# Attention of a perceiver block: four runs of key tiles in place of three, the softmax shift copied under two score tiles of a run, a quarter of the maxima in a score bank

## What is computed

```python
x = x + _L0_xattn_ref(_layernorm(x), ctx_1024, ctx_1024, W_Q, ..., b_O)   # x (32,64,256), ctx (32,1601,256)
x = x + _L0_attn_ref(_layernorm(x), ...)      # state space scan
x = x + _L0_ffn_ref(_layernorm(x), ...)       # top 2 of 8 experts

def _L0_xattn_ref(x_q, x_k, x_v, ...):        # 16 heads of 16
    Q, K, V = (x_q @ W_Q + b_Q), (x_k @ W_K + b_K), (x_v @ W_V + b_V)   # split into heads
    scores = einsum('bhld,bhsd->bhls', Q, K) / sqrt(16)
    return einsum('bhls,bhsd->bhld', softmax(scores), V) ... @ W_O + b_O
```

## Time and profile before

| | us |
|---|---|
| median of 3 runs | 2261.07 (2260.78 to 2264.43) |
| the profiled execution: its own time / its span | 2261.17 / 2259.4 |
| PE busy in the span | 2070.6 (92%) |
| DVE busy | 1453.5 (64%) |
| ACT busy | 1249.6 (55%) |
| POOL busy | 747.9 (33%) |

### The profile page before, as it was taken

How to read it: one execution, slowest core, us unless ns; L and a number is a source line. 1 busy time by engine, 2 the same in 40 slices (tenths; PEclk the granted TensorE clock), 3 DMA queues, 4 the chain that set the end, 5 groups by cost and what they waited for, 6 DMA issues and landing times. The chain is left out here.

```text
span 2259.4 us, 65085 instructions
## 1 busy us (share of the span) xinstructions
PE 2070.6 (92%) x28676; PEld 1738.4 (77%) x28676; DVE 1453.5 (64%) x2619; ACT 1249.6 (55%) x1680; POOL 747.9 (33%) x571
## 2 busy tenths in 40 slices
PE   7999999999999999999999999688699998599993
PEld 5899999988888999999999998543133337599993
DVE  6555665555565565565565563536788874788885
ACT  3455555545555555555555555168799981366661
POOL 3232322222222222222222220000899962255551
PEclk9899999999999999999999999899899998699997
DMA  3111111111111111111111110214875530766663
GB/s 117 38 43 49 41 43 49 41 42 42 45 43 37 49 41 43 49 41 43 49 41 43 49 34 8 66 56 157 233 177 141 144 85 30 232 219 217 226 234 126
DMA packets 131138, 195.41 MB, mean 86 GB/s; under 512 B 18116, under 2 KB 109252, under 8 KB 130696
## 3 DMA queue, kind: packets, MB, share of 16 engines
q1 hardware_dynamic: 121832, 174.98, 25.8%
q0 software_dynamic: 4416, 12.06, 1.6%
q10 hardware_dynamic: 4608, 4.20, 0.6%
HBM read 159.61 MB, written 31.59 MB: 85 GB/s over the span
## 5 line engine op out<-in xcount | busy, mean ns | idle before, releaser
L560 DVE TENSOR_REDUCE max_part<-work 128x1 f32<-128x384 f32 (+1 forms) x1024 | 538.7, 570 | 304.0 <-PE work L692 278.5
L627 ACT ACTIVATE probs<-scores 128x1024 f32<-128x1024 f32 (+1 forms) x416 | 426.1, 1026 | 243.2 <-PE scores L717 222.2
L235 POOL TENSOR_TENSOR ctx_lo<-ctx_whole,ctx_hi 128x768 fp32r<-128x768 f32 (+1 forms) x128 | 232.2, 1815 | 787.4 <-DVE ctx_hi L229 787.4
L1343 POOL TENSOR_TENSOR decay<-steps_in,xn 128x1024 f32<-128x1024 f32 x126 | 243.7, 1964 | 132.9 <-POOLq L951 116.3
L555 DVE SCALAR_TENSOR_TENSOR keys_lo<-work,bk,keys_hi 128x384 fp32r<-128x384 f32 (+1 forms) x256 | 162.7, 635 | 156.4 <-ACT keys_hi L602 156.4
L602 ACT ACTIVATE keys_hi<-work,bk 128x384 fp32r<-128x384 f32 (+1 forms) x256 | 152.5, 596 | 180.2 <-PE work L672 180.2
L711 PE MATMUL scores<-q_hi,keys_hi 64*128 64x256 f32 (+1 forms) x1664 | 247.8, 288 | 2.9 <-issue 1.7
L711 PE MATMUL scores<-q_lo,keys_hi 64*128 64x256 f32 (+1 forms) x1664 | 239.6, 278 | 1.5 <-issue 1.5
L711 PE MATMUL scores<-q_hi,keys_lo 64*128 64x256 f32 (+1 forms) x1664 | 238.8, 278 | 0.0
L682 PE MATMUL work<-wv_hi,ctx_hi 128*128 128x256 f32 (+1 forms) x832 | 235.7, 283 | 1.9
L682 PE MATMUL work<-wv_hi,ctx_lo 128*128 128x256 f32 (+1 forms) x832 | 233.5, 281 | 0.0
(11 more groups left out here) (233 smaller groups left out, 4598.2 us busy)
## 6 DMA issues: line engine op xcount, KB each, us to landing
xs<-in_w_T SPq DMA_DIRECT2D x46, 1024.0 KB, 6.9
ctx_whole<-in_ctx_T SPq DMA_DIRECT2D x96, 384.0 KB, 3.2
steps_in<-scratch_results SPq DMA_DIRECT2D x256, 128.0 KB, 2.7
ctx_whole<-in_ctx_T SPq DMA_DIRECT2D x32, 449.0 KB, 3.8
scratch_results<-steps SPq DMA_DIRECT2D x16, 512.0 KB, 2.6
scratch_mixed<-mixed ACTq DMA_DIRECT2D x32, 128.0 KB, 1.7
scratch_z<-z SPq DMA_DIRECT2D x16, 256.0 KB, 3.7
zg<-scratch_z SPq DMA_DIRECT2D x16, 256.0 KB, 3.1
```

The source lines that it names most:

```text
L235: nc.gpsimd.tensor_tensor(s.ctx_lo[c][:, :, 0:n], s.ctx_whole[c % 2][:, :, 0:n], s.ctx_hi[c][:, :, 0:n].bitcast(F32), ALU.subtract).then_i ...
L560: nc.vector.reduce_max(max_part[par][:, place(pair), c:c + 1], bank[:, 0:CHUNKS[c][1]], AX) \
L627: nc.scalar.activation(probs[n % PROBS][0:rows, :], scores[slot][0:rows, :], ACT.Exp, scale=1.0 / HD ** 0.5).then_inc(exp_done, 1)
L1343: nc.gpsimd.tensor_tensor(decay[u % DS][:, :, 0:n], steps_in[t % LOADS][:, 0:1, 0:n].to_broadcast([P, 2, n]), a_rep[:, 2 * i:2 * i + 2, 0: ...
```

## The change

There are four runs now, one to a chunk: tiles 0 to 2, 3 to 5, 6 to 8, and 9 to 12. A pair of maxima stands in front of the first and the second tile of a run only. Behind the run stand the third pair and a "wide" unit: the fourth pair of maxima goes into the score bank that the run's last tile but one has left (two halves of 512 columns, which are filled whole; the chunk's first columns come from two further small matmuls in chunk 0, from the neighbouring keys in the others), and DVE reduces it in one instruction. `neg_max` is taken behind the last wide unit. Key units of chunk 1 are no longer among the first units.

The shift goes another way for 7 of the 13 tiles. At a batch's start PE writes the two shift matmuls into the bank of tile 1; ACT copies that bank into SBUF (`shift_all`), and tile 1's score adds onto it. For tiles 4, 3, 7, 6, 10 and 9 (the first two tiles of each later run) ACT copies `shift_all` into the score bank (`prefill`), and the score adds onto that; these scores wait for `prefilled` in place of the exponential. Tiles 0, 2, 5, 8, 11 and 12 have their shift matmuls as before.

The core of the diff:

```diff
-FIRST_UNITS = keys_unit(0, 0) + keys_unit(1, 0) + keys_unit(0, 1) + keys_unit(1, 1) + values_unit(0, 1)
+FIRST_UNITS = keys_unit(0, 0) + keys_unit(1, 0) + values_unit(0, 1)
 PHASES = [
-    ([0, 1, 2, 3], [maxima(0, 0, 2), maxima(0, 2, 4), maxima(0, 4, 6), maxima(0, 6, 8)],
-     maxima(1, 0, 2) + keys_unit(0, 2) + keys_unit(1, 2) + values_unit(2) + values_unit(3, 4) + values_unit(5)
-     + values_unit(6, 7)),
...
-    ([8, 9, 10, 11, 12], [maxima(2, 4, 6), maxima(2, 6, 8), maxima(3, 0, 2), maxima(3, 2, 4), maxima(3, 4, 6)],
-     maxima(3, 6, 8) + values_unit(11, 12) + [None, None, ("row",)]),
+    ([0, 1, 2], [maxima(0, 0, 2), maxima(0, 2, 4), []],
+     maxima(0, 4, 6) + wide_maxima(0, 6) + keys_unit(0, 1) + keys_unit(1, 1) + values_unit(2) + values_unit(3, 4) + [None]),
+    ([3, 4, 5], [maxima(1, 0, 2), maxima(1, 2, 4), []],
+     maxima(1, 4, 6) + wide_maxima(1, 6) + keys_unit(0, 2) + keys_unit(1, 2) + values_unit(5) + values_unit(6, 7)),
...
+    ([9, 10, 11, 12], [maxima(3, 0, 2), maxima(3, 2, 4), [], []],
+     maxima(3, 4, 6) + wide_maxima(3, 6) + values_unit(11, 12) + [("row",)]),
 ]
...
+WIDE_TILE = [tiles[-2] for tiles, _, after in PHASES if any(unit and unit[0] == "wide" for unit in after)]
+SHIFT_TILE = PHASES[0][0][1]
+PREFILLED = [t for tiles, _, _ in PHASES[1:] for t in (tiles[1], tiles[0])]
...
+            def wide_unit(b, par, u):
+                _, pairs, c = UNITS[u]
+                dve.wait_ge(wide_done, b * len(WIDE) + WIDE.index(u) + 1)
+                nc.vector.reduce_max(
...
+            def prefill(b, par, t):
+                act.wait_ge(shift_copied, b + 1)
+                act.wait_ge(exp_done, b * NT + t - 1 + CREDIT)
+                if t - 2 in WIDE_TILE and b + 1 < batches:
+                    act.wait_ge(wide_reduced, (b + 1) * len(WIDE) + WIDE_TILE.index(t - 2) + 1)
+                nc.scalar.copy(scores[(par * NT + t) % 2][:, :], shift_all[:, :]).then_inc(prefilled, 1)
+
             def attend(b, par):
+                act.wait_ge(shift_ready, b + 1)
+                nc.scalar.copy(shift_all[:, :], scores[(par * NT + SHIFT_TILE) % 2][:, :]).then_inc(shift_copied, 1)
...
+                    if tiles[-1] + 2 in PREFILLED:
+                        prefill(b, par, tiles[-1] + 2)
                     if b + 1 < batches:
                         for u in after:
                             unit(b + 1, 1 - par, u)
+                            if KIND[u] == "k" and UNITS[u][1] == KD - 1:
+                                prefill(b, par, tiles[-1] + 1)
...
+            def wide_unit(b, par, u):
+                _, pairs, c = UNITS[u]
+                bank = wide_bank(par, u)
+                if b > 0:
+                    pe.wait_ge(exp_done, (b - 1) * NT + WIDE_TILE[WIDE.index(u)] + 1 + CREDIT)
...
             def score(b, par, t):
...
-                pe.wait_ge(exp_done, b * NT + t + 1)
+                ahead = t == SHIFT_TILE or t in PREFILLED
+                if t == SHIFT_TILE:
+                    pe.wait_ge(shift_copied, b + 1)
+                elif t in PREFILLED:
+                    pe.wait_ge(prefilled, b * len(PREFILLED) + PREFILLED.index(t) + 1)
+                else:
+                    pe.wait_ge(exp_done, b * NT + t + 1)
...
+                if not ahead:
+                    last = shift(b, par, t, rows, start=False)
                 last.then_inc(scores_ready, 1)
...
             def attend(b, par):
+                wait_evacuated(pe, b, ROW)
+                pe.wait_ge(exp_done, b * NT + SHIFT_TILE + 1)
+                shift(b, par, SHIFT_TILE, P, start=True).then_inc(shift_ready, 1)
```

More of the change, by code:

```diff
@@ L424 @@
 KIND = [unit[0] if unit else None for unit in UNITS]
+IN_WORK = [kind not in (None, "wide") for kind in KIND]
+WIDE = [u for u in range(NU) if KIND[u] == "wide"]
 ROW = KIND.index("row")
 LAST_MAX = max(u for u in range(NU) if KIND[u] == "max")
+assert WIDE[-1] == LAST_MAX + 1
 WORK_BANKS = 3
-assert NU % WORK_BANKS == 0
+PLACE = [sum(kind != "wide" for kind in KIND[:u]) for u in range(NU)]
+assert sum(kind != "wide" for kind in KIND) % WORK_BANKS == 0
+WORK_OF = [n % WORK_BANKS for n in PLACE]
 BESIDE = []
@@ L438 @@
 V_UNITS = [u for u in range(NU) if KIND[u] == "v"]
-NUMBER = [sum(kind is not None for kind in KIND[:u]) for u in range(NU)]
-DONE = sum(kind is not None for kind in KIND)
-FORMER = [max(i for i in range(u + NU) if i % WORK_BANKS == u % WORK_BANKS and i < u + NU and KIND[i % NU])
+NUMBER = [sum(IN_WORK[:u]) for u in range(NU)]
+DONE = sum(IN_WORK)
+FORMER = [max(i for i in range(u + NU) if WORK_OF[i % NU] == WORK_OF[u] and i < u + NU and IN_WORK[i % NU])
           for u in range(NU)]
@@ L657, in unit @@
                     return
+                if KIND[u] == "wide":
+                    wide_unit(b, par, u)
+                    return
                 kind = KIND[u]
-                bank = work[u % WORK_BANKS]
+                bank = work[WORK_OF[u]]
                 batches_back, former = 1 - FORMER[u] // NU, FORMER[u] % NU
@@ L698, in unit, with shift @@
                 last.then_inc(unit_done, 1)
+            def shift(b, par, t, rows, start):
+                bank = scores[(par * NT + t) % 2]
+                for h in range(2):
+                    last = nc.tensor.matmul(bank[0:rows, h * BANK:(h + 1) * BANK], ones[side(h), 0:rows],
+                                            shifts[side(h), :], start=start, stop=True, skip_group_check=True)
+                return last
             def score(b, par, t):
@@ L711, in score @@
                             last = nc.tensor.matmul(bank[0:rows, at:at + GCOLS], k[par][side(g), m, start:start + rows],
[L712 removed]
+                                                    q[par][side(g), m, :], start=(m == 0 and n == 0 and not ahead),
+                                                    stop=(ahead and m == KD - 1 and n == len(parts) - 1),
                                                     skip_group_check=True)
[L714 to L718 removed]
+                if not ahead:
+                    last = shift(b, par, t, rows, start=False)
                 last.then_inc(scores_ready, 1)
```

79 lines of the change are left out of this document (53 added, 26 removed).

## The result

| | before | after |
|---|---|---|
| median, us | 2260.93 (4 runs, 2259.96 to 2264.43) | 2299.01 (4 runs, 2297.68 to 2300.02) |
| ratio | | 1.0165, 95% interval 1.0148 to 1.0183 |
| span of the profiled execution | 2259.4 | 2298.0 |

The account below looks back on a forecast made before the run. PE was taken to set the pace, waiting in hand-overs once shift pairs no longer filled them. +1.5 us a batch gave +47 over 31 steps, plus 6 for the last batch: 2261 + 47 + 6 = 2314 us, range 2270 to 2346.

Parts of the forecast that it names:

- Hand-over, third tiles: Third tiles of runs 2 to 4: 0.89 us of work against a 1.38 hand-over, waiting 0.49 each, 1.47 a batch.
- First run: Tile 1 waits 0.43 for the shift copy behind ACT's DMA issue, tile 2 0.27 more: 0.70; 0.5 without that hold.
- ACT behind a run: A score-bank write ahead of `keys_hi` delays PE behind the key units: +0.35 in run 2, +0.15 in run 1, total 0.5.
- the dear writes: Rival: ACT needs 1.5 us per write into PSUM, +0.5 each where copies bind, giving 2363 us; chance 0.04.
- A fourth run: One more change from maxima to keys, values to mixes and mixes to maxima, 0.07 to 0.1 each: +0.25 a batch.
- Row unit: At the batch's end the row unit still waits 0.9, now for DVE instead of ACT's values copy: change 0.
- The value units' wait for maxima: Value units' wait for DVE's maxima goes, since the wide unit stands between: -0.3 us a batch.
- Tile 12 and wide: Run 4's fourth tile and the wide unit behind it wait 0.24 us more, exponentials starting no closer than 0.96 apart.
- Wide maxima: Pairs of 512 columns cost 0.23 in place of 0.18, chunk 0's two further matmuls about 0.2: +0.35 a batch.
- The sum: All terms together: +1.5 us a batch, +47 over 31 steps, and +6 in the last batch from exposed ACT copies.
- The clock: Rival: PE's clock falls at each batch's end, costing 2 us a batch, giving 2376 us; chance 0.03.
- The first batch's units hold the same work, 0: The units run in the first batch hold the same work as before, so its time changes by 0.

Follow-up runs that it names:

- e4_nopre: The changed kernel with shift matmuls back in every tile and no ScalarE writes; four runs, wide maxima and pair places kept: 2286.73 us, 1.0114 of before.
- e1_third: The changed kernel with the third pair of narrow maxima of each run moved back in front of the run's third tile: 2282.69 us, 1.0096 of before.
- e3_early: The changed kernel with tile 1's shift matmuls and their copy for the next batch placed ahead of the last run's mixes: 2303.16 us, 1.0188 of before.
- e2_behind: The changed kernel with both ScalarE writes of the score banks placed behind the run's two key units: 2284.51 us, 1.0102 of before.
- e7_runs: The kernel before with four runs and chunk 1's key units moved as in the changed kernel; narrow maxima, all 13 shift pairs on PE: 2255.85 us, 0.9971.
- r1_before: The kernel before run once more, unchanged: 2265.32 us (1 run).
- r2_after: The changed kernel run once more, unchanged: 2299.29 us (1 run).
- e10_row: e7_runs with the last run's mixes and ACT's copy of `mixed` ahead of the row unit and first units: 2234.96 us, 0.9894 of before.
- e13_first: e10_row plus ScalarE writes only for each later run's first tile, behind the key units, and the copied shift made in tile 0's bank: 2244.28 us, 0.9935 of before.
- e12_wide: Changed kernel, third pair before third tile, writes behind key units, shift copy before mixes, plus wide units of runs 1 to 3 behind key units: 2291.53 us, 1.0137.

## Why the prediction came out

- *Hand-over, third tiles.* Right: 1.38 to 1.40 from a score's end to full pace on the tile two later, so a wait of 0.49, of which the list shows 0.23 and not 0.3 to 0.5. That shift pair and maxima had filled the time is shown by e4_nopre (with six shift pairs back the period is even 0.20 shorter) and e1_third (the waits at third tiles go from 114 to 4).
- *First run.* 0.70 was predicted, 0.45 + 0.21 = 0.66 measured, with the copy behind the DMA's issue. e3_early shows that the smaller figure of the prediction, 0.5 without that hold, is the floor: its third tile starts at 732.03, 1.28 behind the first score's end; with the 0.10 of its slower first pair this is the 1.38 of the hand-over alone.
- *ACT behind a run.* 0.5 predicted; 0.42 by the trace and 0.46 by e2_behind. The write was guessed at 1.0 us and takes 1.017; the dear writes fell.
- *A fourth run.* 0.25 predicted, 0.27 by e7_runs.
- *Row unit.* Right: 0.7 as before, now for `neg_max`. The value units' wait for maxima went as said, and 448 shift matmuls stand in place of 832.
- *Tile 12 and wide.* 0.24 predicted, about 0.2 found.
- *Wide maxima.* 0.35 predicted, of which 0.2 for chunk 0's two further matmuls. No run shows this term alone, but those 0.2 are too much: in e4_nopre run 1, which has them, takes 4.07 from its maxima to its keys, and run 2 takes 4.04.
- *The sum.* +1.5 a batch predicted, 43.89 - 42.28 = +1.61 measured; last batch +6 predicted, 26.34 - 20.80 = +5.5 measured (+4.4 against r1_before, whose last batch is slower; see the clock).
- *The clock.* 1.00 in the window of after, so that rival fell. The section on HAM oscillation in the Trainium skill (TensorE: Matmul & The Clock Gate) has a kernel that loses the clock at each of its waits for DMA. The batches here keep 1.00 in spite of the waits listed above, so it doesn't show in them. The 1.00 of the last batch in the earlier trace rows, which the prediction held against this rival, isn't there in every execution. Windows of r1_before, at its last batch's start:

```profile
1398.00:1401.00 3.00, 1.32 (x58) 1.04 (x47) 0.00 (x0) 0.32 (x1) 0.00 (x0) 1.00 0.00 0
1401.00:1404.00 3.00, 3.00 (x36) 2.70 (x34) 0.00 (x0) 1.88 (x3) 0.00 (x0) 0.68 0.16 49
```

Behind a stretch in which PE is busy 1.32 of 3 us the granted clock falls to 0.68; in the first profile of before PE is busy 1.52 of 3 us there, and 1.00 follows. What decides stays open.

The forecast was 15 us too high, and two steps of the total are mis-sized. "The first batch's units hold the same work, 0": the first copy of `mixed` comes at 113.7 in place of 121.5 (113.9 against 123.6 in the repetition), 8 to 10 us earlier. And the 31 steps were added to a time of before that holds more than 31 periods: in nine batches of before PE stops, 11 us together (last section), and after has almost none. The 29 steps of after are 35.9 us longer in all, which is 29 x 1.61 = 46.7 less what those stops had added; the batch behind them adds 2.0, the last 5.5, the part after the attention 3.0; less 7.8 this is the 38.6 by which the span grew. The prediction has nothing for that part. The 3.0 comes again as 2.1 in the second pair (r2_after against r1_before); over the fourteen profiles the part takes 838.7 to 841.5 in before, r1_before, e7_runs, e10_row and e13_first and 842.5 to 846.6 in the others. Whether and how the change lengthens it stays open. What the forecast's mechanism covers comes to 46.7 + 2.0 + 5.5 = 54.2, close to the 53 forecast; the first batch, the stops and the later part lie outside it.

## What to carry over

Matmuls that fill the time of a hand-over cost little; before moving them to another engine, measure the hand-over from the end of one piece to full pace on the next, and count only what lies outside it. Of 1.38 us of shift pairs a batch the best form kept 0.13, and each fill that was taken away uncovered the next chain (the second exponential and, as far as the trace tells, DVE's reductions). The time lay in the order: independent mixes between a producer and the unit that waits for it gave 0.8% on top of the four runs (0.9894 against 0.9971).

## What the runs showed of the hardware

**PE stops at the same instructions.** In two executions of the kernel before, PE stopped for something that the profile doesn't show, with the same number of matmuls of the tile left. Timeline of r1_before, and of the first profile of before:

```profile
377.85 0.51 PE L731 MATMUL acc<-probs,values 65*17 65x64 f32 x19 [0.57 <-issue]
...
421.40 0.41 PE L731 MATMUL acc<-probs,values 65*17 65x64 f32 x14 [0.67 <-issue]
...
465.43 0.38 PE L731 MATMUL acc<-probs,values 65*17 65x64 f32 x10 [1.48 <-issue]
```

```profile
375.46 0.51 PE L731 MATMUL acc<-probs,values 65*17 65x64 f32 x19 [0.67 <-issue]
...
418.97 0.41 PE L731 MATMUL acc<-probs,values 65*17 65x64 f32 x14 [0.65 <-issue]
...
462.56 0.38 PE L731 MATMUL acc<-probs,values 65*17 65x64 f32 x10 [1.05 <-issue]
```

> The kernel before once more, unchanged, to see whether the stops of PE inside the last run's mixes (waits for nothing that the profile shows, batches 6 to 14 of the first profile, 0.6 to 1.4 us each, 11 us together) come again at the same places. My theory (they belong to the program: where its instructions lie): the same ten batches take 43.1 to 44.3 in place of 42.28, total steady time 1275 to 1276. Rival (they belong to one execution): other batches or none, 1264 to 1268.

> The changed kernel once more, unchanged, for the same question and for the 3 us that its part after the attention took longer. Theory (the program's): no stops, every batch 43.9, first copy of mixed values at 113.7, tail 3 us longer than that of the kernel before in the same call. Rival (one execution's): some batches with stops, another tail.

Both came as the theories had it, r1_before with 1277 us of steady time for the 1275 to 1276 expected. In both executions the place is the program's: matmuls 19, 14, 10, then 5 and 1 from the end of the tile's mix, each batch four or five later. The extent repeats in sum, 10.8 and 11.9 us, nearly all in the same nine batches (behind the fifth the stops fall among the scores), though not batch by batch: the ninth distance is 43.96 in one and 45.67 in the other. After has 0.6 and 0.3. What PE waits for there stays open.

**The clock in the first batch.** Granted clock between 50 and 80 us, where the first units run (windows of r1_before, e4_nopre and e7_runs; that of after is above, 1.00):

```profile
50.00:80.00 30.00, 28.22 (x106) 21.86 (x106) 16.46 (x33) 5.79 (x11) 5.52 (x3) 0.72 0.19 55
```

```profile
50.00:80.00 30.00, 28.10 (x295) 23.81 (x295) 19.92 (x37) 12.40 (x20) 7.22 (x4) 1.00 0.15 43
```

```profile
50.00:80.00 30.00, 27.91 (x153) 22.65 (x153) 17.49 (x34) 9.46 (x16) 5.53 (x3) 0.83 0.16 42
```

1.00 is the level of 2.4 GHz; means between come from parts at 1.2. The kernels with the wide unit ahead of the key units stand at 0.94 to 1.00 here, those with narrow maxima alone at 0.72 to 0.89, and e12_wide, with the wide unit behind the key units, at 0.89. The first copy of the first group comes 5 to 11 us earlier than that of before, r1_before or e7_runs. That PE's waits for DVE's single reductions lower the clock is argued from this, not shown by a run of its own, and how much of the earlier copy is the clock's and how much DVE's shorter work isn't separated.
